# Vision tower on one core: the front rebuilt with one half ahead, one sum of squares for two norms, and attention with 88-token value chunks

## The chip, the cores and the metric

The kernel runs on one core of one Trainium2 chip. The metric is device time in microseconds (us), lower is better.

## The reference, cut to what matters

```
h = patches @ W + b + pos, two class tokens in front        # 8 images, S = 66 tokens, D = 192
a = layernorm(h)                                            # "complex" attention, 12 heads of 16
sr = (qr kr' + qi ki') / 4 ; si = (qi kr' - qr ki') / 4
h = h + softmax(sqrt(sr*sr + si*si)) @ v
x = layernorm(h); r = x                                     # the encoder's input
for i in range(4):                                          # 4 layers
    nx = rmsnorm(r, ln1[i])
    q, k, v = nx @ attn_q[i], nx @ attn_k[i], nx @ attn_v[i]    # 12 heads of 64
    r = r + softmax(q k' + bias) @ v @ attn_o[i]
    nx = rmsnorm(r, ln2[i])
    y = relu(nx @ ffn_wi[i]) @ ffn_wo[i]                    # inner width 768
    if i in (1, 3): y += top-2 mixture of 8 experts (gelu)
    r = r + y
out = h + rmsnorm(r, ln_f)
```

## The kernel before, in words

All state lies transposed, features on partitions, tokens along the row. The 8 images are two halves of 4 images (264 tokens), and the halves leapfrog: while one half does softmax, the other half gives TensorE products. Every fp32 product of a weight with an activation is made of five fp32r products (`split_pairs`): weights and activations are split in a high and a low part. The weights come from HBM in chunks (`split` stages): SyncE loads `raw`, ScalarE writes the high part (`high_part`), GpSimd the low part (`low_parts`, three or four pieces), and only then may TensorE use the chunk.

What is done when is written out by hand in `stages()`, one list of stages. Each of the five engines walks through the same list and does its own part of every stage, strictly in that order. So an engine that waits in one stage also holds up its own part of all the later ones. PSUM banks are handed around in list order as well: three banks `pa` (copied out by ScalarE), three `pd` (by VectorE), two `ps` (scores); the hidden products of the feed-forward (`hid`) take `pa` and `ps` banks, which VectorE frees.

The stages that matter here, each for a half `hf` and mostly for one image `b`:

- `cproj`, `cscores`, `croot`, `cexp`, `ctp`, `cvals`, `cpv`: projection, the two score parts and their squares, root and maximum, exponential with sum and scale, transpose, values, and product with the values, all of the complex attention in the front.
- `mean`, `squares`, `norm`, `scale`: a norm. `squares` is ScalarE's, `norm` sums the squares on TensorE (12 tiny products), VectorE adds epsilon, GpSimd takes the power -0.5 (`inverse_root`), and `scale` spreads the root over the partitions on TensorE, after which VectorE scales and splits x (`split_x`).
- `qk` (six product groups for q and six for k), `scores`, `tp`, `pv`, `o_tail`, `o_main`: attention of a layer. The softmax of one image takes VectorE (bias added to two halves of the heads, maximum), GpSimd (maximum subtracted), ScalarE (exponential, `exps`), VectorE (sum and reciprocal), GpSimd (scaled), TensorE (`tp`), in this order. In a `scores` stage for b > 0 the exponential, the sum and the scaling are those of image b - 1; `scores_end` does them for the last image.
- `v`: the values, made with tokens on partitions: `xs` as the stationary operand, 66 tokens of one image, and 384 columns of the weights stream past, 10 products an image; ScalarE copies them to `vtok`.
- `logits`: the router of the mixture, a chain of some 25 short VectorE instructions.
- `warm(n)`: n products of zeros on TensorE where it would be idle otherwise.

The front does both halves of each step one after the other and ends with both attention outputs; then layer 0 begins. The encoder's layernorm and the first `ln1` norm are two norms in series. In the layers without experts (0 and 2) both halves' attention is interleaved image by image (`scores`, `pv`, `v`, with `warm(2)`). In layers 1 and 3 each half does `scores` and `v` of its four images alternately, then `hid`, then `tp` and `pv` among parts of the other work.

## Time and profile before

| what | us |
|---|---|
| median of 3 runs | 766.58 (756.33 to 770.01) |
| the profiled execution, its own time | 758.47 |
| its span, first to last instruction | 755.7 |
| TensorE matmul busy | 704.8 (93%) |
| TensorE weight load busy | 626.9 (83%) |
| VectorE busy | 445.1 (59%) |
| ScalarE busy | 406.6 (54%) |
| GpSimd busy | 352.2 (47%) |
| mean granted TensorE clock | 0.972 of full speed |

Matmul busy counts pipelined instructions from start to end, so 93% does not mean peak speed, and it includes the 191 `warm` products, which compute nothing. Time is lost where the order makes an engine wait; the rows further down show the stretches.

### The profile page before, as it was taken

What the parts mean: (1) busy time and instruction counts of PE and PEld (TensorE: products, weight loads), DVE (VectorE), ACT (ScalarE), POOL (GpSimd) and SP (SyncE); (2) the same over time, 40 slices, a digit from 0 to 9 for tenths busy, and PEclk for the clock granted to TensorE, in tenths of its full rate; (3) what the DMA queues carried; (4) which work ended last, traced back from release to release, by engine and by line L of the source; (5) the groups of instructions that cost most, each with busy time, mean ns of one, the idle gap of its engine ahead of it and who ended that gap; (6) DMA issues with size and microseconds to landing.
All of it is one profiled execution on the core that took longest, in us unless ns stands there. A gap on an engine that the chain in (4) does not pass through costs nothing.

```text
span 755.7 us, 16388 instructions
## 1 busy us (share of the span) xinstructions
PE 704.8 (93%) x6735; PEld 626.9 (83%) x6735; DVE 445.1 (59%) x941; ACT 406.6 (54%) x913; POOL 352.2 (47%) x327
## 2 busy tenths in 40 slices
PE   6976999899899999899999999998999999999995
PEld 4853578788787989899999888887889898999995
DVE  0348435386556486676556645764765865666664
ACT  1387335542456365677767355444554647767642
POOL 2357525472466244336675333515743533544520
PEclk9997899998999999999999999989999999999998
DMA  7321001020220204243345030002211134233200
GB/s 211 88 74 43 2 2 33 1 85 1 69 78 18 59 3 131 81 126 116 119 143 147 3 84 1 2 2 74 74 43 33 28 105 123 83 116 91 89 1 22
DMA packets 36609, 49.20 MB, mean 65 GB/s; under 512 B 6155, under 2 KB 27575, under 8 KB 36023
## 3 DMA queue, kind: packets, MB, share of 16 engines
q1 hardware_dynamic: 33259, 43.49, 20.1%
q10 hardware_dynamic: 3276, 4.67, 2.0%
q8 instruction: 53, 0.87, 0.5%
q14 instruction: 21, 0.17, 0.1%
HBM read 47.70 MB, written 0.45 MB: 64 GB/s over the span
## 4 chain that ended last, share of the span: by engine, by line
PE 72%; DVE 9%; ACT 8%; POOL 5%; issue 3%; DMA 2%; SPq 0%; POOLq 0%; ACTq 0%; DVEq 0%
PE pd L684 35%; PE pa L684 23%; PE ps L684 9%; PE pa L715 4%; POOL w L613 1%; DVE xn L1102 1%; POOL prob L622 1%; ACT wide L1022 1%; POOL wo L613 1%; ACT w L934 1%; ACT wqkv L934 1%; DVE xs L1072 1%; DVE xs L1074 1%; ACT pa L1023 1%; ACT csq L983 1%
## 5 line engine op out<-in xcount | busy, mean ns | idle before, releaser
L613 POOL TENSOR_TENSOR w<-raw,w 128x384 fp32r<-128x384 f32 x140 | 141.8, 1015 | 132.0 <-ACT w L934 124.1
L684 PE MATMUL pd<-wide,w 128*128 128x264 f32 x1200 | 156.0, 286 | 0.1
L684 PEld LDWEIGHTS pd<-wide,w 128*128 128x128 f32 x1200 | 149.2, 188 | 0.9 <-DVE wide L1250 0.9
L684 PE MATMUL pa<-xs,w 128*128 128x264 f32 x810 | 120.7, 289 | 10.3 <-DVE wide L1250 6.6
L684 PEld LDWEIGHTS pa<-xs,w 128*128 128x128 f32 x810 | 107.1, 190 | 14.9 <-DVE wide L1250 8.6
L1250 DVE TENSOR_TENSOR wide<-pa,wide 128x264 fp32r<-128x264 f32 x144 | 62.1, 432 | 40.4 <-ACT pa L1023 38.0
L622 POOL TENSOR_TENSOR prob<-prob,mx 66x792 f32<-66x792 f32 x36 | 55.4, 1543 | 45.9 <-DVE mx L1062 45.6
L1022 ACT ACTIVATE wide<-pa 128x264 fp32r<-128x264 f32 x144 | 56.8, 394 | 35.0 <-PE pa L684 34.8
L628 POOL TENSOR_TENSOR prob<-prob,rc 66x792 f32<-66x792 f32 x36 | 54.4, 1513 | 44.1 <-DVE rc L1068 44.1
L684 PE MATMUL ps<-xs,w 128*128 128x264 f32 x480 | 74.3, 285 | 0.5 <-DVE prob L1227 0.5
L613 POOL TENSOR_TENSOR wqkv<-raw,wqkv 128x384 fp32r<-128x384 f32 x48 | 49.6, 1034 | 48.0 <-ACT wqkv L934 45.2
L1138 DVE TENSOR_TENSOR pd<-pd,vtok 128x264 f32<-128x264 f32 x64 | 43.6, 681 | 39.5 <-PE pd L684 39.4
L684 PE MATMUL pa<-xs,wqkv 128*128 128x264 f32 x480 | 61.7, 287 | 4.7 <-DVE xs L1074 4.0
L684 PEld LDWEIGHTS ps<-xs,w 128*128 128x128 f32 x480 | 64.6, 188 | 1.3 <-issue 1.2
L684 PEld LDWEIGHTS pa<-xs,wqkv 128*128 128x128 f32 x480 | 59.3, 188 | 7.6 <-DVE xs L1074 6.6
L684 PE MATMUL pa<-wqkv,xs 128*66 128x384 f32 x320 | 63.5, 345 | 0.0
L684 PE MATMUL pd<-warm_x,warm_w 128*128 128x512 bf16 x191 | 59.2, 429 | 0.0
L902 ACT ACTIVATE qk<-pa 128x264 f32<-128x264 f32 x102 | 39.4, 390 | 36.8 <-PE pa L684 36.5
L634 POOL TENSOR_TENSOR rs<-var,exponent 88x3 f32<-88x3 f32 x22 | 18.7, 849 | 85.6 <-DVE var L1084 85.6
L1023 ACT ACTIVATE pa<-pa 128x264 f32<-128x264 f32 x144 | 56.6, 393 | 0.0
L934 ACT ACTIVATE w<-raw 128x1536 fp32r<-128x1536 f32 (+1 forms) x40 | 52.6, 1321 | 7.4 <-PE pd L684 3.9
L1006 ACT ACTIVATE vtok<-pa 66x384 f32<-66x384 f32 x64 | 29.8, 482 | 46.5 <-PE pa L684 46.4
(126 smaller groups left out, 1149.4 us busy)
## 6 DMA issues: line engine op xcount, KB each, us to landing
raw<-in_moe_w_dram SPq DMA_DIRECT2D x16, 576.0 KB, 4.2
raw<-in_moe_w_dram SPq DMA_DIRECT2D x16, 384.0 KB, 3.5
raw<-in_moe_w_dram SPq DMA_DIRECT2D x32, 192.0 KB, 3.9
vtok<-cw_rows ACTq DMA_DIRECT2D x4, 1056.0 KB, 6.0
raw<-in_attn_o_dram SPq DMA_DIRECT2D x4, 576.0 KB, 4.0
raw<-in_ffn_wo_dram SPq DMA_DIRECT2D x4, 576.0 KB, 4.1
vtok<-in_patches_dram SPq DMA_DIRECT2D x2, 768.0 KB, 7.9
raw<-in_attn_q_dram SPq DMA_DIRECT2D x4, 384.0 KB, 3.6
```

Source lines behind the costliest of these rows:

```text
L613: ins = nc.gpsimd.tensor_tensor(low, whole, high.bitcast(F32), ALU.subtract)
L622: nc.gpsimd.tensor_tensor(p, p, m.unsqueeze(2).to_broadcast([S, H, S]), ALU.subtract).then_inc(sub_ready, 1)
L628: nc.gpsimd.tensor_tensor(p, p, r.unsqueeze(2).to_broadcast([S, H, S]), ALU.mult).then_inc(prob_ready, 1)
L684: return nc.tensor.matmul(out_ap, lhsT, rhs, start=first, stop=last)
L715: last = nc.tensor.transpose(bank[0:S, j * S:(j + 1) * S], probs(u)[:, g * HG + j, :], ident[0:S, 0:S])
L902: nc.scalar.activation(dst, src, ACT.Copy).then_inc(a_free, 1)
L934: nc.scalar.activation(hi, src, ACT.Copy).then_inc(chunk_hi, 1)
L1006: nc.scalar.activation(vtok[0:S, hf * HALF_B + b, n * F // 2:(n + 1) * F // 2], bank_a()[0:S, 0:F // 2], ACT.Copy).then_inc(a_free, 1)
L1022: nc.scalar.activation(wide[hf][:, 0, m, :], bank, gate_fn)
L1023: nc.scalar.activation(bank, bank, gate_fn).then_inc(h_ready, 1)
L1138: done(nc.vector.tensor_tensor(part, part, weight, ALU.mult))
L1250: nc.vector.tensor_tensor(wide[hf][:, 1, m, :], places["h"][n][0][:, 0:NT], wide[hf][:, 0, m, :].bitcast(F32), ALU.subtract).then_inc(h_fr ...
```

## The change

1. Scores: the products of the two 64-row groups (even and odd heads) now alternate, one from each, into two banks, where before six of one group were followed by six of the other.
2. Values: 3 chunks of 88 tokens (`VCN`) for a half instead of 4 images of 66 tokens. ScalarE copies a chunk to a staging tile (`v_rows`), waits for its copies, and issues two DMAs that carry the rows to their images in `vtok`; `pv` waits for `v_moved`. Staging lies over `wide` (half 0) or `qk` (half 1), and half 1's q and k lie over its `wide` (`qk_late`).
3. Norm: the encoder's layernorm and the `ln1` of layer 0 use one sum of squares; the variance of the second follows from that of the first. GpSimd takes both roots in one stage, x goes through `sq`, and the copy `h1T` moves from ScalarE to GpSimd.
4. Front: the raw complex weights have a place of their own, so SyncE loads the first two weight chunks at once, and their `split` stages come before `cproj`. A small Sqrt at the start brings ScalarE's table in, and a `sqrt_table` stage does so once more. Half 0 goes through the whole complex attention first; half 1's scores come after it and the rest of half 1's (`croot` 2 and 3, `cexp`, `ctp`, `cpv`, norm) in layer 0.
5. Order in the layers: `scores` stages are spread out between `v`, `qk` and `hid`; in the expert layers `scores` of image 3 comes after `logits` (half 1) or after the first `tp` (half 0), and `scores_end` after the `w1` split. The `warm` products fall from 191 to 93: layers 0 and 2 from 32 each to 14 and 11, layers 1 and 3 from 18 to 13, the front from 91 to 42.
6. Small: gate and value weights are doubled onto all 128 rows and halved by ScalarE; `cvals` is one stage an image.

The diff, cut to its core:

```diff
@@ the expert layers, half 1 (half 0 is similar)
-        for b in range(HALF_B):
-            yield ("scores", 1, layer, b)
-            if b == 0:
-                yield ("scale", 0, "ln2", layer)
-            yield ("v", 1, layer, b)
-        yield from hid(0, layer, 0)
+        yield ("scores", 1, layer, 0)
+        yield ("v", 1, layer, 0)
+        yield ("scale", 0, "ln2", layer)
+        yield ("v", 1, layer, 1)
+        yield ("scores", 1, layer, 1)
+        yield ("v", 1, layer, 2)
+        yield ("hid", 0, layer, 0, 0)
+        yield ("scores", 1, layer, 2)
+        yield ("hid", 0, layer, 0, 1)
         yield ("logits", 0, layer)
         yield ("tp", 1, layer, 0)
-        yield ("scores_end", 1, layer)
+        yield ("scores", 1, layer, 3)
         yield ("split", None, "w1", layer, 1)
         yield ("cw_out", 0, layer)
         yield ("y_tail", 0, layer, 0)
         yield ("pv", 1, layer, 0)
         yield ("tp", 1, layer, 1)
+        yield ("scores_end", 1, layer)
@@ layer 2 (layer 0 from its second block of half 1 on)
+                yield from qk(0, layer)
+                yield ("scores", 0, layer, 0)
+                yield ("v", 0, layer, 0)
+                yield ("norm", 1, "ln1", layer)
+                yield ("v", 0, layer, 1)
+                yield ("scores", 0, layer, 1)
+                yield ("scale", 1, "ln1", layer)
+                yield ("v", 0, layer, 2)
+                yield ("scores", 0, layer, 2)
+                yield ("qk", 1, layer, 0)
+                yield ("tp", 0, layer, 0)
+                yield ("scores", 0, layer, 3)
+                yield ("pv", 0, layer, 0)
+                yield ("qk", 1, layer, 1)
+                yield ("tp", 0, layer, 1)
+                yield ("scores_end", 0, layer)
+                yield ("pv", 0, layer, 1)
...
@@ PE, scores
-                    for g in range(2):
-                        bank = bank_s()
-                        row = slice(DK * g, DK * g + DK)
-                        for j in range(HG):
-                            last = mm(bank[0:S, j * S:(j + 1) * S], qk[row, 0, j, cols], qk[row, 1, j, cols], True, True)
-                        last.then_inc(s_full, 1)
+                    pair = [bank_s(), bank_s()]
+                    for j in range(HG):
+                        for g in range(2):
+                            row = slice(DK * g, DK * g + DK)
+                            last = mm(pair[g][0:S, j * S:(j + 1) * S], qk_of[hf][row, 0, j, cols], qk_of[hf][row, 1, j, cols], True, True)
+                            if j == HG - 1:
+                                last.then_inc(s_full, 1)
@@ ACT, v
+                    rows_of = v_rows(hf, layer)
                     for n in range(2):
-                        nc.scalar.activation(vtok[0:S, hf * HALF_B + b, n * F // 2:(n + 1) * F // 2], bank_a()[0:S, 0:F // 2],
+                        nc.scalar.activation(rows_of[:, c, n * F // 2:(n + 1) * F // 2], bank_a()[0:VCN, 0:F // 2],
                                              ACT.Copy).then_inc(a_free, 1)
+                    act.wait_ge(a_free, groups_after(A_GROUPS, stage))
+                    for b, to, at, rows in V_MOVES[c]:
+                        act.dma_start(vtok[to:to + rows, hf * HALF_B + b, :], rows_of[at:at + rows, c, :]).then_inc(v_moved[hf][b], 16)
@@ DVE, norm
+                if kind == "encoder":
+                    nc.vector.tensor_scalar(var_enc[:, :], sums, EPS_LN, None, ALU.add)
+                    nc.vector.tensor_scalar(var[:, :], sums, 1.0 + EPS_RMS, EPS_RMS * EPS_LN, ALU.mult, ALU.add).then_inc(d_free, 1)
```

## Rows read from the trace of the kernel before

**Rows 1.** The page, busy time, share of the span and instructions of each engine.

```profile
PE 704.8 (93%) x6735; PEld 626.9 (83%) x6735; DVE 445.1 (59%) x941; ACT 406.6 (54%) x913; POOL 352.2 (47%) x327
```

**Rows 2.** Timeline of TensorE, layer 1, half 0: start, us, what, idle before.

```profile
214.09 1.47 PE L684 MATMUL ps<-qk 64*66 64x66 f32 x24
215.49 1.95 PE L684 MATMUL pa<-wqkv,xs 128*66 128x384 f32 x10
217.37 1.47 PE L684 MATMUL ps<-qk 64*66 64x66 f32 x24
...
235.35 0.92 PE L684 MATMUL pd<-probT,vtok 66*64 66x66 f32 x24
...
244.71 0.80 PE L684 MATMUL pd<-ident,rs 88*128 88x88 f32 x6
...
246.29 1.47 PE L684 MATMUL pd<-warm_x,warm_w 128*128 128x512 bf16 x6
247.87 3.91 PE L684 MATMUL pa<-xs,wqkv 128*128 128x264 f32 x30
```

**Rows 3.** Timeline of TensorE, the front and layer 0's two ends.

```profile
75.70 1.74 PE L684 MATMUL pd<-vtok,xn 128*66 128x192 f32 x4 [4.94 <-DVE vc L1193]
...
91.51 0.67 PE L684 MATMUL pd<-probT,vc 66*32 66x66 f32 x32
...
93.95 0.71 PE L684 MATMUL pd<-hT,mean_w 128*128 128x264 f32 x2 [0.63 <-DVE hT L1216]
...
110.32 7.64 PE L684 MATMUL pa<-xs,wqkv 128*128 128x264 f32 x60
...
204.98 3.92 PE L684 MATMUL pa<-xs,wqkv 128*128 128x264 f32 x30 [1.52 <-DVE xs L1074]
```

**Rows 4.** Groups by line and form: busy us, mean ns, idle before and its releaser.

```profile
L1227 DVE TENSOR_TENSOR prob<-ps,bias 66x396 f32<-66x396 f32 x64 | 32.7, 550 | 20.5 <-PE ps L684 20.3
L1062 DVE TENSOR_REDUCE mx<-prob 66x12 f32<-66x792 f32 x36 | 34.8, 973 | 4.1 <-ACT prob L990 3.0
L1067 DVE TENSOR_REDUCE rc<-prob 66x12 f32<-66x792 f32 x36 | 34.8, 966 | 31.9 <-ACT prob L914 31.9
L622 POOL TENSOR_TENSOR prob<-prob,mx 66x792 f32<-66x792 f32 x36 | 55.4, 1543 | 45.9 <-DVE mx L1062 45.6
L613 POOL TENSOR_TENSOR w<-raw,w 128x384 fp32r<-128x384 f32 x140 | 141.8, 1015 | 132.0 <-ACT w L934 124.1
L634 POOL TENSOR_TENSOR rs<-var,exponent 88x3 f32<-88x3 f32 x22 | 18.7, 849 | 85.6 <-DVE var L1084 85.6
L914 ACT ACTIVATE prob<-prob 66x792 f32<-66x792 f32 x36 | 30.9, 863 | 24.3 <-POOL prob L622 23.8
```

**Rows 5.** Busy time by stretch (PE, PEld, DVE, ACT, POOL), granted clock, DMA.

```profile
76.00:82.00 6.00, 6.00 (x25) 2.85 (x23) 2.59 (x5) 1.75 (x3) 4.10 (x3) 0.50 0.02 4
```

**Rows 6.** The same view, later stretch, end of layer 2's attention.

```profile
501.00:506.00 5.00, 5.00 (x39) 3.34 (x39) 3.33 (x7) 0.00 (x0) 0.00 (x0) 0.56 0.02 3
```

**Rows 7.** Timeline of TensorE: first products of layers 2 and 3.

```profile
433.78 2.09 PE L684 MATMUL pa<-xs,wqkv 128*128 128x264 f32 x15 [0.29 <-DVE xs L1074]
...
522.55 3.92 PE L684 MATMUL pa<-xs,wqkv 128*128 128x264 f32 x30 [1.53 <-DVE xs L1074]
```

**Rows 8.** Timeline of ScalarE's queue, one issue of a transfer.

```profile
282.51 0.58 ACTq L1030 DMA_DIRECT2D cw_rows<-cw  x1
```

**Rows 9.** The DMA view: weight loads, KB each, median us to landing.

```profile
raw<-in_moe_w_dram SPq DMA_DIRECT2D x32, 192.0 KB, 3.9
```

**Rows 10.** Timeline of TensorE, layer 1, half 1: first scores, first expert's hid.

```profile
259.85 1.47 PE L684 MATMUL ps<-qk 64*66 64x66 f32 x24
...
290.41 0.88 PE L684 MATMUL ps<-xs,w 128*128 128x264 f32 x5
```

**Rows 11.** Timeline of VectorE: first and last instruction of a router.

```profile
278.80 0.18 DVE L1114 COPY lg<-pd 88x24 f32<-88x24 f32 x1 [0.20 <-PE pd L684]
...
282.30 0.18 DVE L1132 TENSOR_TENSOR cw<-cw,lg 88x24 f32<-88x24 f32 x1
```

More of the change, by code:

```diff
@@ L92, in stages @@
     yield ("norm", 1, "complex", 0)
-    yield from warm(6)
-    for part in range(3):
-        yield ("cproj", 0, part)
-        if part == 0:
-            yield ("scale", 1, "complex", 0)
+    yield from warm(4)
     yield ("split", None, "qkv", 0, 0)
     yield ("split", None, "qkv", 0, 1)
+    yield ("cproj", 0, 0)
+    yield ("scale", 1, "complex", 0)
+    yield ("cproj", 0, 1)
+    yield ("cproj", 0, 2)
     for b in range(HALF_B):
         yield ("cscores", 0, b)
-        if b < 3:
-            yield ("cproj", 1, b)
-        else:
-            yield ("split", None, "qkv", 0, 2)
@@ L132, in stages @@
+    yield ("cpv", 0, 2)
     yield ("ctp", 0, 3)
-    yield from warm(2)
-    yield ("cpv", 0, 2)
-    yield ("cexp", 1, 2)
-    yield from warm(2)
+    yield ("cvals", 1, 2)
+    yield ("cvals", 1, 3)
     yield ("cpv", 0, 3)
     yield ("mean", 0, "encoder")
-    yield ("cexp", 1, 3)
+    yield ("split", None, "qkv", 0, 2)
+    yield from warm(2)
     yield ("squares", 0, "encoder")
+    yield ("cscores", 1, 0)
+    yield ("norm", 0, "encoder", 0)
+    yield ("cscores", 1, 1)
     yield from warm(2)
-    yield ("ctp", 1, 0)
@@ L162, in stages @@
-    yield from warm(2)
-    yield ("cpv", 1, 2)
-    yield from warm(2)
-    yield ("cpv", 1, 3)
+    yield ("scale", 0, "ln1", 0)
+    yield ("croot", 1, 0)
+    yield ("cscores", 1, 2)
+    yield ("croot", 1, 1)
+    yield ("scale", 0, "encoder", 0)
+    yield ("cscores", 1, 3)
+    yield from warm(4)
     for layer in range(LAYERS):
@@ L174, in stages @@
                 yield ("squares", 1, "encoder")
-                beside = [[("norm", "encoder", 0)], [("scale", "encoder", 0), ("squares", "ln1")], [("norm", "ln1", 0)], [("scale", "ln1", 0)]]
-            else:
-                beside = [[("norm", "ln1", layer)], [("scale", "ln1", layer)], [], []]
-            for b in range(HALF_B):
-                yield ("scores", 0, layer, b)
-                for x in beside[b]:
-                    yield (x[0], 1) + x[1:]
-                yield ("v", 0, layer, b)
@@ new lines, in stages @@
+                yield ("scores", 0, 0, 3)
+                yield ("tp", 0, 0, 0)
+                yield from warm(3)
+                yield ("scale", 1, "ln1", 0)
+                yield ("scores_end", 0, 0)
+                yield ("split", None, "o", 0, 0)
+                yield ("pv", 0, 0, 0)
+                yield ("scale", 1, "encoder", 0)
+                yield ("qk", 1, 0, 0)
+                yield ("tp", 0, 0, 1)
+                yield from split_block(0, 0)
+                yield ("pv", 0, 0, 1)
@@ L215, in stages @@
             yield ("squares", 0, "ln1")
+            yield ("tp", 1, layer, 3)
+            yield from warm(2)
+            yield ("pv", 1, layer, 3)
             yield ("o_tail", 1, layer)
@@ L493, in x_ready_after, with roots_after @@
             return sum(x[0] == "scale" and x[2] in ("complex", "ln1", "ln2") for x in order[:order.index(stage) + 1])
+        def roots_after(norm_stage):
+            return sum(1 + (x[2] == "encoder") for x in order[:order.index(norm_stage) + 1] if x[0] == "norm")
         def bank_places():
@@ L1235, in _ @@
                 elif name == "pv":
+                    if hf == 0 and stage[3] == 0 and stage[2]:
+                        for b in range(HALF_B):
+                            dve.wait_ge(v_moved[0][b], 16 * V_PARTS[b] * (stage[2] + 1))
                     w = wide[hf][:, :, :, stage[3] * S:(stage[3] + 1) * S]
```

313 lines of the change are left out of this document (173 added, 140 removed).

## The prediction

> **What bounds the kernel now.** I read the page first: TensorE is busy 93% of the span, the next engine 59% [rows 1]. So far TensorE seems to be the bound, but the view of stretches tells another story for the front: from 76 to 82 us the granted clock is 0.50, that is the lower of its two levels, 1.2 GHz [rows 5], after 4.9 us idle [rows 3], and part of the busy time is warm products. Then I walked its timeline with the groups by line beside it. In the expert loops product follows product, and the change doesn't touch them. In attention an image costs 1.40 us of scores and 1.88 of values (the distances of the starts) [rows 2], 3.3 in all. Its softmax costs VectorE 2 x 0.55 + 0.97 + 0.97, with the reciprocal 3.3, and GpSimd 2 x 1.5 [rows 4]. So three engines are in balance there: to take work from TensorE alone shows only where the order puts something else beside the softmax.
>
> **The sum is made against the profiled execution**, 758.5 us (span 755.7). The median of the runs shown is 8.1 above it, and I add that at the end, taking the runs after to scatter as those before.
>
> **Work that TensorE loses.** Values: 10 products of 384 columns fewer in each of 8 half-layers, 1.88 each, 15.0 us [rows 2]. Scores: 24 instructions take 1.47 from start to end, with one row group after the other. The trace has no 64-row alternation; the nearest row is `pv`, 24 instructions of the same 66 columns alternating between two column groups, 0.92 [rows 2]. With that 0.55 are saved an image, 17.6 for 32. The ends are nothing (the two groups don't overlap) and the rate of `cpv`, 32 in 0.67 over four column groups [rows 3], hence 0.50 for 24 and 31 in all; I take `pv`'s, as it has two groups as well. Warm products: 98 fewer, 1.47/6 = 0.24 each at most [rows 2], 24 us; these are worth something only where nothing was waited for. Together 56 us, and the question is how much of it comes back as waiting.
>
> A rule of the Trainium skill speaks against the second term. "TensorEngine Tiling (Array Packing)", section Instruction Overhead, gives each matmul some 60 cycles of overhead and advises not to take the tiling factor from a dimension that is already small; 66 columns are such. By it alternating would save next to nothing; the rows of `pv` and `cpv` speak for overlap. It is a rival below.
>
> **Layer 2, walked stage by stage** (88.8 us from its first product to layer 3's [rows 7]). TensorE loses 8 x 0.55 for scores, 2 x 1.88 for values and 21 warm products (0.22 from start to start), 4.5, together 12.7. The order then makes it wait: `qk` of half 1 needs its scaled x, which before came 4 us or more behind `scale` (3.2 us from `scale` to `qk` where VectorE is free [rows 2], some 2 more where a maximum and a sum stand before it in VectorE's list [rows 4]), and now only a value chunk and one scores stage (2.7) lie between, 3.0; `pv` right behind its own `tp`, 0.5; the norm and the `scale` of half 0 before `hid` with less warm, 1.2 each; image 3 of half 1 now after `y`, where `o_tail` waits for VectorE to empty `pv`, 1.7. That is 7.6. In return the stretch at half clock, 501 to 506 us [rows 6], loses its 9 warm products and the small waits about it, 4.8. Net 9.9 faster. The bounds are 5 (the clock falls for the same work) and 14 (no new wait).
>
> **Layers 1 and 3.** TensorE loses 4.4 + 3.8 + 1.1 = 9.3 in each. Half 0 between 214 and 248 us: `v` 2 now needs a `pa` bank that `hid` took, and VectorE frees it only after the sum of image 0, since `scores` 1 precedes `hid` in its list; `tp` 0 likewise waits for `scores` 2's maximum and sum. I come to `tp` 0 some 1.8 us earlier than before and to scores 3 at 232.3. From there GpSimd decides: bias and maximum 2.1, subtract 1.5, scaling of image 2 1.5, `w1` split 4 x 1.02 (in the list now ahead of `scores_end`), scaling of image 3 1.5, root 0.85 [rows 4], which ends at 243.9. The scale before stood at 244.7 [rows 2]. So a gain of 0.7 of the 4.7 removed. Half 1, from the first scores to the first expert's `hid` 30.6 us before [rows 10]: scores 3 now stands behind the router on VectorE, 3.7 us [rows 11], then bias, maximum and sum 3.3, and GpSimd again does subtract, scale, `w1` split and scale, 8.6. My walk ends at 293.3 against 290.4, so 2.9 slower. A layer with experts is 2.2 slower, both 4.4. The bounds are 5 faster and 5 slower each: the longest chain runs over five engines, and 3 us of its links are waits that I could only place to within a microsecond.
>
> **The moves of the values.** 48 DMAs on ScalarE's queue, 0.58 each to issue [rows 8], behind a wait for its own copies: 1.2 us an image chunk in which the exponentials and bank copies queued behind on ScalarE stand still. It is in the walks above (exponentials 1.1 later). A move is up to 66 rows of 3,072 bytes, 203 KB; loads of 192 KB land in 3.9 [rows 9]. Between a chunk's issue and its first `pv` lie 4 to 10 us in every half, so it costs nothing at 3.9, and at twice that about 2 us in each of 8 half-layers.
>
> **The front.** Half 0's first `qk` begins at 110.3 before, and its `mean` at 93.95 [rows 3]. Walked anew: the two high parts (2 x 1.4) leave ScalarE's way ahead of the first squares, 2.4 gained; four images of scores, squares, root and maximum take 2.5 each on ScalarE and VectorE, until 46; then exponentials and sums of half 0 alone, scale 1.5 each on GpSimd, `tp` and `pv` among projections of half 1, until 66.8, which is 27 before the old 93.95. From the mean to `qk` one norm instead of two: squares, 12 sums, variance, root 0.85, 5.5 in all. `qk` at 77.7, 32.6 earlier. Against it: between 38 and 75 us TensorE has short bursts, and [rows 5] show half clock around such work; some 15 us of products there can take twice their time, most hidden behind ScalarE. I set 6 us for it and for two-input VectorE operations beside GpSimd. With this 26.6.
>
> **Layer 0**, 94.7 before [rows 3]. It loses 4.4 + 3.8 + 18 x 0.22 = 12.2 and half 1's second norm; it gets half 1's roots, exponentials, transposes and products (5.2 on TensorE). GpSimd must subtract and scale half 1's images before the first `ctp`: about 5 us of TensorE idle behind `v` 0, another 1.5 at half 1's norm. I walk it to 89.7, so 5.0 gained. The front's work for half 1 is thus paid here in part; both together 31.6.
>
> **Sum.** 26.6 + 5.0 + 9.9 - 4.4 = 37.1 faster. 758.5 - 37.1 = 721.4 for an execution like the profiled one, 729.5 beside the median; as two of three runs before lie high and more may lie low after, I say 728.
>
> **The rivals.**
> (a) The layers with experts gain too: the waits that I placed behind the router and the `w1` split hide in what TensorE still has. Then 5 a layer instead of -2.2, 14 more: 714. For it: the walk's waits of 1 to 3 us each all hang on the same few links. Chance 0.18.
> (b) The front gains half: ScalarE, serial through roots, copies and two table changes, or the half clock, set the pace. 16 less: 744. For it: [rows 5]; against: half 0 alone has half of the work. Chance 0.17.
> (c) The row groups don't overlap, the Trainium skill's rule of small dimensions named above. Scores stay at 1.4; of the 17.6 some 10 would have shown, in layers 0 and 2 and some elsewhere: 738. Chance 0.10.
> (d) Slower: the moves land late. `pv` and all that is queued behind it on TensorE and VectorE wait in 8 half-layers; the slack is about 5 us beyond 3.9, so it decides above 9, and each further us costs 8. The gain is gone at 9 + 37/8 = 13.6 us, and at 15 the kernel is 11 slower: 777. Against: the nearest transfer in size lands in 3.9 [rows 9]. Chance 0.04.
> (e) It doesn't do what it says, as the front's warm products held the clock up and their loss lowers it over both dense layers as well: 15 us of gain lost beside (b): 752. Chance 0.05.
>
> **How the numbers follow.** My forecast has 0.46, with a range of its own of 718 to 738 from the bounds above. The range 709 to 746 takes in (a), (b), (c) and leaves out some 0.2. Two per cent of 766.6 is 15.3, about what a measurement of this kernel can tell from no change: faster is below 751. That holds for the forecast, (a), (c), nearly all of (b) and half of (e): 0.88. Slower holds for (d) and the tail of (e): 0.04. The rest, 0.08, is no change.
>
> **What the profile after would show.** `scores` groups of 24 at some 0.9 us instead of 1.47; value products x240; the first `qk` near 80 us; layer 1's first near 173; layer 2's length near 79; layer 1's no shorter than before, with TensorE waiting for GpSimd's scaling before `tp` of image 3, right behind the `w1` split; `v_moved` waits nowhere. I am wrong if layers 1 and 3 shorten by over 3 us each, if the first `qk` comes after 90, or if the granted clock is low in the dense layers over long stretches.

## The result, and the profile after

The kernel after takes 782.17 us (median of 4 runs, 780.09 to 790.22) where the kernel before takes 765.95: ratio 1.027, 95% interval 1.015 to 1.040. So it is slower, clear of no change; whether by 2% or more the interval leaves open. The forecast was 728. Executions of one program differ by 1 to 2%, and the profiled ones of experiments 1 and 7 were among the slower of theirs (spans 770.3 and 754.2). The profiled execution of after took 781.9 with a span of 780.1, 24.4 above the span of before, at a mean granted clock of 0.905 (0.972 before). The page's first part, to be laid beside [rows 1]:

```profile
PE 695.9 (89%) x6533; PEld 635.8 (82%) x6533; DVE 443.0 (57%) x941; ACT 398.4 (51%) x898; POOL 351.8 (45%) x329
```

TensorE is busy only 9 us less, although it has 202 instructions fewer and each scores stage is shorter: part of what was removed came back as products at the lower clock. And for 33 us more of the span it is idle. The view of stretches shows where, cut at the first `qk` of each layer: front, layer 0, 1, 2, 3 with the output. Columns: busy us of PE, PEld, DVE, ACT, POOL, granted clock, DMA share, GB/s. First before:

```profile
0.00:110.32 110.32, 90.78 (x895) 62.86 (x896) 47.66 (x87) 53.15 (x94) 51.31 (x57) 0.91 0.26 72
110.32:204.98 94.66, 88.08 (x907) 75.34 (x905) 52.84 (x100) 42.92 (x86) 45.34 (x38) 0.95 0.11 33
204.98:433.78 228.80, 220.91 (x2021) 207.77 (x2021) 145.24 (x328) 138.83 (x328) 118.46 (x111) 1.00 0.30 87
433.78:522.55 88.77, 83.84 (x882) 72.08 (x882) 52.69 (x98) 39.92 (x82) 37.48 (x30) 0.96 0.10 28
522.55:755.70 233.15, 221.24 (x2034) 208.89 (x2034) 146.71 (x332) 131.73 (x323) 99.59 (x92) 0.99 0.24 68
```

and after:

```profile
0.00:82.18 82.18, 68.65 (x654) 52.00 (x655) 39.70 (x71) 43.64 (x82) 40.73 (x52) 0.94 0.35 96
82.18:197.98 115.80, 99.89 (x1036) 88.16 (x1035) 61.06 (x115) 49.57 (x95) 55.96 (x46) 0.78 0.14 41
197.98:440.92 242.94, 221.89 (x1993) 209.64 (x1992) 144.12 (x328) 137.02 (x324) 118.32 (x111) 0.94 0.30 88
440.92:532.98 92.06, 82.02 (x846) 73.33 (x846) 52.38 (x97) 37.77 (x78) 37.36 (x30) 0.85 0.15 45
532.98:780.10 247.12, 223.42 (x2011) 212.71 (x2009) 145.78 (x332) 130.45 (x319) 99.42 (x92) 0.93 0.24 71
```

The front is 28.1 us shorter (forecast 26.6). Layer 0 is 21.1 longer (forecast 5.0 shorter), layers 1 and 3 are 14.1 and 14.0 longer (2.2 each), layer 2 is 3.3 longer (9.9 shorter).

**Layer 0** first. TensorE's timeline behind the second value product of half 0 (answers to [rows 3]):

```profile
98.14 1.53 PE L781 MATMUL pa<-ident,vtok 66*66 66x66 f32 x12 [4.92 <-POOL vtok L689]
99.61 1.62 PE L750 MATMUL ps<-qk 64*66 64x66 f32 x24
101.16 1.11 PE L750 MATMUL pd<-probT,vc 66*32 66x66 f32 x32
102.19 1.53 PE L781 MATMUL pa<-ident,vtok 66*66 66x66 f32 x12
103.48 3.22 PE L750 MATMUL pa<-wqkv,xs 128*88 128x384 f32 x10
106.63 0.67 PE L750 MATMUL pd<-probT_late,vc 66*32 66x66 f32 x32
107.23 0.88 PE L781 MATMUL pa<-ident,vtok 66*66 66x66 f32 x12
108.04 0.94 PE L750 MATMUL ps<-qk 64*66 64x66 f32 x24
```

and the same place by stretches:

```profile
92.00:97.00 5.00, 1.23 (x8) 0.77 (x6) 4.90 (x9) 3.50 (x5) 4.83 (x4) 0.90 0.00 0
97.00:102.00 5.00, 3.86 (x68) 3.56 (x68) 3.17 (x7) 3.15 (x5) 4.54 (x4) 0.50 0.19 54
102.00:107.00 5.00, 5.00 (x58) 4.08 (x53) 2.53 (x5) 1.75 (x4) 3.98 (x3) 0.58 0.01 3
```

TensorE waits 4.9 us for half 1's first scaled image, and then works at a granted clock of 0.50, that is 1.2 GHz. The price stands in the upper fence, as each group occurs at both levels: scores 1.62 and 0.94, transposes 1.53 and 0.88, `cpv` 1.11 and 0.67; the value products take 3.22 here and 1.95 elsewhere. The five groups from 98 to 107 us lose 3.7. "PE busy 5.00" at a clock of 0.50 is thus half of what it looks like. The same comes at 117 to 127, 162 to 177 and 192 to 197 us of this layer, each time behind a wait (1.6, 2.2 and 1.4 us). In before's layer 0, 16 of 19 stretches of 5 us show 1.00.

**Layer 1, half 0** (answers to [rows 2]). ScalarE:

```profile
210.88 1.59 ACTq L1079 DMA_DIRECT2D vtok<-v_rows_wide  x2
...
214.52 1.56 ACTq L1079 DMA_DIRECT2D vtok<-v_rows_wide  x2
216.13 0.86 ACT L981 ACTIVATE prob<-prob 66x792 f32<-66x792 f32 x1 [1.64 <-issue]
```

VectorE:

```profile
217.03 0.97 DVE L1142 TENSOR_REDUCE rc<-prob 66x12 f32<-66x792 f32 x1 [1.95 <-ACT prob L981]
218.03 0.22 DVE L1143 RECIPROCAL rc<-rc 66x12 f32<-66x12 f32 x1
218.18 0.36 DVE L1331 TENSOR_TENSOR wide<-ps,wide 128x264 fp32r<-128x264 f32 x1
```

TensorE:

```profile
207.18 0.94 PE L750 MATMUL ps<-qk 64*66 64x66 f32 x24
...
219.03 3.44 PE L750 MATMUL pa<-wqkv,xs 128*88 128x384 f32 x10 [3.23 <-DVE wide L1331]
...
227.54 0.85 PE L781 MATMUL pa<-ident,prob 66*66 66x66 f32 x12 [2.20 <-DVE wide L1331]
...
248.55 4.47 PE L750 MATMUL pa<-xs,wqkv 128*128 128x264 f32 x30
```

Read these three against time: the second pair of moves holds ScalarE until 216.1, the exponential starts then, the sum on VectorE waits for it, and behind the sum stand the operations that free `hid`'s banks, which the next value products need. From the first scores to half 1's `qk` it is 41.4 us, before 33.8. A pair of moves costs 1.56 to 1.59, 0.79 an issue, against the 0.58 of [rows 8]; in layer 0 single pairs take up to 2.23.

**Layer 1, half 1** (answers to [rows 10]). GpSimd, then TensorE:

```profile
287.83 4.21 POOL L674 TENSOR_TENSOR w<-raw,w 128x384 fp32r<-128x384 f32 x4
292.01 1.51 POOL L689 TENSOR_TENSOR prob<-prob,rc 66x792 f32<-66x792 f32 x1
```

```profile
293.57 1.53 PE L781 MATMUL pa<-ident,prob 66*66 66x66 f32 x12 [3.47 <-POOL prob L689]
...
295.88 1.59 PE L750 MATMUL pd<-probT,vtok 66*64 66x66 f32 x24
```

The last transposes wait behind the `w1` split, as forecast, and the clock falls there too. The first expert starts 36.3 us behind the first scores (261.13 to 297.40), before 30.6.

### The profile page after: what moved, and what is told of

Read it like the earlier page. It is cut to its first block, busy times and chain, and to the rows that moved or that the text cites. A ratio compares the mean times of both kernels' runs of the same rounds, so it can differ in the third digit from the quotient of the medians.

```text
span 780.1 us, 16044 instructions
## 1 busy us (share of the span) xinstructions
PE 695.9 (89%) x6533; PEld 635.8 (82%) x6533; DVE 443.0 (57%) x941; ACT 398.4 (51%) x898; POOL 351.8 (45%) x329
## 4 chain that ended last, share of the span: by engine, by line
PE 57%; DVE 13%; ACT 10%; POOL 7%; ACTq 4%; issue 4%; DMA 3%; SPq 0%; POOLq 0%; DVEq 0%
PE pd L750 28%; PE pa L750 18%; PE ps L750 7%; PE pa L781 3%; ACTq L1079 3%; POOL w L674 2%; DVE rc L1142 2%; DVE mx L1137 1%; DMA gate<-in_gate_w_dram 1%; ACT prob L981 1%; POOL prob L689 1%; DVE prob L1305 1%; ACT wide L1097 1%; POOL wqkv L674 1%; DVE hT L1233 1%
## 5 line engine op out<-in xcount | busy, mean ns | idle before, releaser
L750 PE MATMUL pa<-xs,w 128*128 128x264 f32 x810 | 124.8, 295 | 9.1 <-DVE wide L1331 5.8
L750 PEld LDWEIGHTS pa<-xs,w 128*128 128x128 f32 x810 | 110.8, 196 | 14.5 <-DVE wide L1331 7.8
L750 PE MATMUL ps<-xs,w 128*128 128x264 f32 x480 | 78.0, 294 | 1.6 <-DVE prob L1305 1.6
L1097 ACT ACTIVATE wide<-pa 128x264 fp32r<-128x264 f32 x144 | 56.6, 393 | 39.8 <-PE pa L750 37.8
L750 PE MATMUL pa<-xs,wqkv 128*128 128x264 f32 x480 | 68.1, 303 | 8.0 <-DVE xs L1149 5.2
L750 PEld LDWEIGHTS pa<-xs,wqkv 128*128 128x128 f32 x480 | 65.4, 205 | 10.3 <-DVE xs L1149 6.5
L750 PEld LDWEIGHTS ps<-xs,w 128*128 128x128 f32 x480 | 68.1, 198 | 2.3 <-issue 1.8
L674 POOL TENSOR_TENSOR wqkv<-raw,wqkv 128x384 fp32r<-128x384 f32 x48 | 49.1, 1023 | 29.4 <-ACT wqkv L1001 26.6
L750 PE MATMUL pa<-wqkv,xs 128*88 128x384 f32 x240 | 50.1, 357 | 6.7 <-DVE wide L1331 5.5
L1305 DVE TENSOR_TENSOR prob<-ps,bias 66x396 f32<-66x396 f32 x64 | 33.3, 560 | 39.9 <-PE ps L750 39.8
L1012 ACT ACTIVATE sq<-hT 128x528 f32<-128x528 f32 x16 | 10.3, 645 | 88.2 <-DVE hT L1223 88.2
L1331 DVE TENSOR_TENSOR wide<-ps,wide 128x264 fp32r<-128x264 f32 x96 | 41.3, 430 | 19.3 <-ACT ps L1098 17.7
## 6 DMA issues: line engine op xcount, KB each, us to landing
vtok<-qk ACTq DMA_DIRECT2D x8, 198.0 KB
```

Source lines behind the costliest of these rows:

```text
L674: ins = nc.gpsimd.tensor_tensor(low, whole, high.bitcast(F32), ALU.subtract)
L750: return nc.tensor.matmul(out_ap, lhsT, rhs, start=first, stop=last)
L1097: nc.scalar.activation(wide[hf][:, 0, m, :], bank, gate_fn)
L1305: nc.vector.tensor_tensor(prob[:, b, heads, :], bank_s()[0:S, 0:HG * S].rearrange("p (h n) -> p h n", h=HG), bias[:, heads, ::-1], ALU.add ...
L1331: nc.vector.tensor_tensor(wide[hf][:, 1, m, :], places["h"][n][0][:, 0:NT], wide[hf][:, 0, m, :].bitcast(F32), ALU.subtract).then_inc(h_fr ...
```

## The experiments

The forecast had named waits and the clock as what could go wrong, and had charged the moves with little. The theories tested: **clock** (fewer zeros and more waits put TensorE at the lower clock), **order** (the new order of the lists makes it wait), **moves** (staging and moving the values costs more than 80 products). Ratios are to the kernel before, run on the same chip; the experiments ran on four chips, so across the groups 1 to 8, 9 to 12, 13 to 15 and 16 to 18 the ratios tell more than the times.

**1. Zeros where the kernel after waits.** 220 of them, 55, 60, 45 and 60 in the four layers; the first of layer 0:

```
                 yield ("cexp", 1, 3)
+                yield from warm(20)
                 yield ("ctp", 1, 0)
```

> The changed kernel with 220 more products of zeros (313 instead of 93), put where TensorE waits in its layers. Theory clock (the removed products and the new waits let the granted clock fall to its lower level over the attention stretches, 70 us of half-rate loss by the stage table): the mean clock comes back from 0.905 to 0.96 or more and the time falls from 782 to 745 or less. Theory order (the chains through VectorE and GpSimd set the time, the clock only follows): the added products hide nothing and the time stays within 1% of 782 or rises.

764.1 us, ratio 1.006 (1.002 to 1.010): 18 less than after by work that computes nothing. Layer 0 takes 111.0 (115.8), layer 2 86.1 (92.1), at a clock of 0.97 instead of 0.85. The clock is part of the cause, but not all of it: the forecast of this theory was 745, and layer 1 stays at 239.8 with its clock back at 0.99.

**2. Fewer zeros in the kernel before.** 50 of its 191 taken away, in its layers, such as

```
-            yield from warm(6)
             yield from qk(1, layer)
```

> The kernel before with 50 of its 191 products of zeros taken from its layers (141 left), nothing else changed. Theory clock: the clock falls in layers 0 and 2 and the time rises by 5 to 20 us though work is removed. Theory order: the products were either hidden or on the path, so the time is the same or up to 10 us lower.

757.6, ratio 0.993 (0.989 to 0.997), layer clocks 0.96, 1.00, 0.98, 0.98. These 50 zeros weren't what kept the clock up; in this order, without long waits, they are superfluous.

**3. Only the alternating scores, in the kernel before.**

```
+                    pair = [bank_s(), bank_s()]
+                    for j in range(HG):
+                        for g in range(2):
+                            last = mm(pair[g][...], ...)
```

> The kernel before with the score products alternating between the two row groups, nothing else. If they overlap as they do in the changed kernel (24 in 0.94 us instead of 1.47), 17 us of TensorE time go; theory clock expects less than 10 of them to show, as shorter bursts bring more waiting and perhaps a lower clock; theory order expects 5 to 12, as VectorE needs 3.3 us an image and TensorE then 2.8.

757.1, ratio 0.989 (0.986 to 0.993). A scores stage takes 0.94, as forecast (0.92), but of 17 us of shorter stages some 8 show in the time (5 to 11 by the interval). The profiled executions don't show where: the four layers together are 1.4 us shorter there, layer 1 228.2 for 228.8. That the softmax of the same image takes up the rest is argued from the order and not shown.

**4. The kernel after with layers 1 to 3 in the order and with the zeros of before.** Front, layer 0, 88-token values, moves and scores stay.

> The changed kernel (new front, new layer 0, 88-token values, alternating scores, shared norm) with layers 1 to 3 in the order of the kernel before and their products of zeros back (124 in all). Theory order: layers 1 and 3 come back to 228 to 233 us or less each and layer 2 to 85 or less, time 745 to 755. Theory moves (the wait and two issues of 1.6 us a chunk on ScalarE's queue cost more than the products that they save): layers 1 to 3 stay slower than before by 3 us or more each.

The zeros are 124 in all. 754.9, ratio 0.989 (0.985 to 0.993): 27 less than after. Layers 230.1, 91.0, 234.7; layer 0 still 114.0 at a clock of 0.78.

**5. The kernel after without moves** (values by image, copied straight to `vtok`):

```
-VC, VCN = 3, NT // 3
+VC, VCN = HALF_B, S
```

> Kernel after, but the values are computed as before, an image of 66 tokens at a time, and copied straight to their place: 80 products of 384 columns more, no staging and none of the 48 moves. If the moves (two issues of 1.56 us a pair on ScalarE, and waits behind them) cost more than the products they save, it comes out 8 to 15 us faster than after, about 770, with layers 1 and 3 at 238 each. If the order alone is what costs, TensorE's 15 us of products are added back and it takes 782 to 795.

772.7, ratio 1.012 (1.005 to 1.018). It has 15 us of products more and is 9 us faster. Layer 1, half 0, from the first scores to half 1's `qk`: 35.1 (after 41.4). In layer 3 the same stretch didn't get shorter: 38.2 (after 37.8).

**6. Experiments 4 and 5 together.**

> The kernel after with layers 1 to 3 in the order of before (the fourth experiment, 754.9 us) and in addition the values by image without moves. That experiment differs from the kernel before with alternating scores, in layers 1 to 3, by the 88-token chunks and their moves alone. If the moves cost: layers 1, 2 and 3 fall from 230.1, 91.0 and 234.7 to 228, 88 and 233, and the whole to about 749. If they cost nothing and the products are dear, 755 to 765.

749.3, ratio 0.982 (0.975 to 0.989). Layers 227.6, 86.7 and 232.8, so the moves cost 2.5, 4.3 and 1.9 there. Only the last two are clear of scatter: with nothing changed in them, layer 1 took 227.6 to 230.8 and layer 2 83.9 to 88.3 (at clocks of 1.00 to 0.94) in experiments 11, 12, 14, 17 and 18. Against the fifth, the order of layers 1 to 3 with its zeros is worth 23 us.

**7. The fourth with 55 zeros more, all in layer 0.**

> The fourth experiment (new front and new layer 0, old order in layers 1 to 3) with 55 products on zeros more, all in layer 0, where TensorE waits there: 20 of them ahead of the first transposes of half 1's complex attention, where it idles 3.8 us and then shows a granted clock of 0.50 for 10 us. If the low clock is what makes layer 0 take 114 us, it falls to 104 or less and the whole to 745. If the waits themselves (for GpSimd and VectorE) set its length, it stays at 110 or more and the clock alone rises.

748.8, ratio 0.980 (0.973 to 0.987). Layer 0 110.6, clock 0.89: 3 to 6 us back of the 20, the clock mostly repaired. The stretch up to half 1's `qk` takes 40.1 at a clock of 0.97, in the fourth 45.6 at 0.76. (The wait of 3.8 in the expectation is the idle part of one window of 5 us; the row of the fourth's trace has 4.92.)

**8. The fourth with real work in the wait**, `("v", 0, 0, 1)` moved ahead of `("ctp", 1, 0)`.

> The fourth experiment with one stage moved: in layer 0 the second chunk of half 0's values (about 3 us of TensorE's work) stands ahead of the first transposes of half 1's complex attention, into the wait for GpSimd of 3.8 us, instead of behind them. If the idle time is what lowers the clock, that wait shrinks below 1.5 us, the stretch at 0.50 behind it goes, and layer 0 takes 108 instead of 114. If not, the clock stays low there and layer 0 gains at most 2.

756.0, ratio 0.992 (0.988 to 0.997). A miss. Nothing gained:

```profile
96.20 1.10 PE L776 MATMUL pa<-wqkv,xs 128*88 128x384 f32 x5 [1.10 <-ACT v_rows_first L1101]
99.16 0.54 PE L807 MATMUL pa<-ident,vtok 66*66 66x66 f32 x6 [1.86 <-POOL vtok L715]
100.86 0.87 PE L807 MATMUL pa<-ident,vtok 66*66 66x66 f32 x6 [1.17 <-ACT v_rows_first L1101]
```

The products' bank copies stand behind the exponentials on ScalarE, so the wait of 4.9 became three of 4.1 in all, and the clock is 0.50 from 102 to 117 us. Layer 0 takes 117.1.

**9. The kernel after, its moves issued by SyncE.**

```
-                    act.wait_ge(a_free, groups_after(A_GROUPS, stage))
-                    for b, to, at, rows in V_MOVES[c]:
-                        act.dma_start(...)
...
+                elif stage[0] == "v":   # in SyncE's program
+                    sp.wait_ge(a_free, groups_after(A_GROUPS, stage))
+                    for b, to, at, rows in V_MOVES[c]:
+                        sp.dma_start(...)
```

> Kernel after, with one thing changed: the 48 moves of the values are issued by SyncE, at the same place of the order, and not by ScalarE. Bytes, landing and all else stay. If the moves cost because ScalarE stands still for their issue (1.56 us a pair) and the exponentials and copies queued behind come late, the 6.3 us that half 0 of layer 1 is longer than without moves go (41.4 to 36 or less), and the whole is at or below the 772.7 of the kernel without moves: 765 to 773. If they cost because they land late, nothing changes: 780 to 784.

769.3, ratio 1.013 (1.006 to 1.020). The same as the fifth within the intervals, with all moves made: the issue on ScalarE was the price and not the landing. (SyncE, which loads the weights, now follows the list too, so a load can stand behind a chunk's copies.) The exponential that began at 216.13 in after begins at 212.19 here, counted from the first scores 2.9 earlier, and

```profile
215.93 1.95 PE L760 MATMUL pa<-wqkv,xs 128*88 128x384 f32 x10 [1.20 <-DVE wide L1338]
```

waits 1.2 where it waited 3.2, and runs at the full clock. It begins 9.8 behind the first scores instead of 11.9. Half 0 takes 37.5, and 36.4 in layer 3.

**10. The sixth with the new order in half 1 of layers 1 and 3 alone** (`hid` between the scores, scores 3 behind the router, `w1` split ahead of the end of the scores).

> The sixth experiment (old order in layers 1 to 3, values by image, 749.3 us) with half 1's attention in layers 1 and 3 alone in the order of after: hid between the scores, scores 3 behind the router, the w1 split ahead of the end of the scores. The trace of the fifth experiment has 34.5 us from half 1's first scores to the first expert against 30.0 in the sixth. If that stretch alone makes the difference, each expert layer is 4.5 to 7 longer here: 234 and 239, the whole 759 to 763. If half 0's order is what costs, both stay within 2 of 227.6 and 232.8.

760.5, ratio 1.000 (0.997 to 1.004), 11 more than the sixth (1.8% by the ratios); layers 1 and 3 are 234.9 and 240.0, which is 7.3 and 7.2 longer. The last wait, at the `w1` split:

```profile
281.94 0.88 PE L809 MATMUL pa<-ident,prob 66*66 66x66 f32 x12 [2.28 <-POOL prob L717]
```

**11. The sixth with the second half of layer 0 in the old order.**

> The sixth experiment with layer 0 changed from half 1's second norm on: half 1's qk in one piece, scores, transposes and values one image after another with zeros ahead, the tail as before, as in layer 2 of before. If the new order of this part is what lengthens layer 0 (the granted clock is 0.50 from 122 to 132, 162 to 177 and 187 to 197 us there), layer 0 falls from 116.1 to 108 or less and the whole to 741. If half 1's complex attention ahead of it is what costs, it stays at 114 or more.

747.9, ratio 0.982 (0.976 to 0.989), layer 0 115.4: no change in the sum, but two changes that cancel. From half 1's `qk` on it takes 66.8 (72.0 in the sixth, 65.8 in before). The stretch ahead of it takes 48.6 (44.1): the edit also moved the split of the output weights ahead of `qk`, beside VectorE's work on half 1's x, and the clock is low there. So the new order does cost in this part, and this run doesn't clear it.

**12. The eleventh with 26 zeros in layer 0's first part.**

> The eleventh experiment with 26 products on zeros more in the first part of layer 0: 20 ahead of the first transposes of half 1's complex attention, 6 ahead of its norm. If each long wait is followed by a stretch at the lower clock and zeros prevent it, layer 0 falls by another 4 to 6 us, to 104, and the whole to 737. If zeros only stand in the way, it is no faster than the eleventh.

741.6, ratio 0.973 (0.966 to 0.980): faster than both kernels. Layer 0 110.8, clock 0.91; up to half 1's `qk` 42.7, in the eleventh 48.6. The stretches that stood at 0.90, 0.50 and 0.58 in after:

```profile
92.00:97.00 5.00, 4.93 (x37) 2.89 (x35) 4.73 (x7) 4.97 (x8) 3.75 (x3) 1.00 0.00 0
97.00:102.00 5.00, 4.39 (x85) 3.05 (x84) 4.33 (x9) 2.74 (x5) 5.00 (x4) 1.00 0.00 0
102.00:107.00 5.00, 5.00 (x118) 4.04 (x116) 3.13 (x8) 3.49 (x7) 4.53 (x4) 1.00 0.02 3
```

**13. The kernel after, roots first.** `croot` 2 and 3 of half 1 ahead of half 0's first `qk`, its first two `cexp` between the parts of `qk`.

> Kernel after, with four stages moved in layer 0: the roots of half 1's complex images 2 and 3 ahead of half 0's first qk, and the exponentials of its images 0 and 1 between the two parts of qk, not behind its scores. On ScalarE they then don't stand behind the 12 copies of qk, which end at 90.3 us in the trace of after; VectorE and GpSimd are idle 6.8 and 8.8 us for them. If layer 0 is long because half 1's chain (root, maximum, subtraction, exponential, scale, transposes) starts behind qk's copies, the wait of 4.9 us before the first transposes goes, with it the clock of 0.50 from 97 to 107 us, and layer 0 takes 109 or less instead of 115.8, the whole 772 to 776. If the chain's own work sets the end, or the clock falls anyway, layer 0 stays above 113.

782.9, ratio 1.027 (1.020 to 1.034); layer 0 116.3. A miss: the wait of 4.9 is gone, and 0.8 and 1.9 in `qk` (its copies now stand behind roots and exponentials) and 3.7 before `cpv` are there instead.

**14. The same in the twelfth.**

> The twelfth experiment (741.6 us, layer 0 110.8 at a mean clock of 0.91) with the same four stages moved. If the chain's late start is the cause, layer 0 takes 104 to 107 and the whole 735 to 738. If not, 740 to 743.

746.2, ratio 0.981 (0.972 to 0.989); layer 0 115.2, longer than the twelfth's 110.8. Refuted here as well.

**15. The fourteenth with 88-token values, moved by SyncE.**

> The fourteenth experiment with the values in 88-token chunks again and their moves issued by SyncE: 80 value products of 384 columns fewer (15 us of TensorE), and the wait for a landed move before the product with the values. In the order of after this was 3.4 us faster than no moves (769.3 against 772.7). If the moves cost only by their issue on ScalarE, it is 3 to 8 faster than the fourteenth. If they also land late for the old order, or TensorE's saved time turns into idle time and a lower clock, it is the same or up to 5 slower.

745.9, ratio 0.983 (0.975 to 0.992), the same as the fourteenth. TensorE is busy 9 us less (670.8 for 679.9) and nothing of it shows in the times; the layers of the profiled executions are each 0.4 to 0.5 us shorter. So even with the moves off ScalarE the 88-token chunks are worth nothing that can be measured here. (The 3.4 us of the expectation compare two chips; by their ratios, 1.013 and 1.012, the ninth and the fifth don't differ.)

**16. The kernel after, less work in GpSimd's list.** For half 1's complex images it subtracts the maximum from one head of twelve:

```
+                if HALF_B <= u < B:
+                    nc.gpsimd.tensor_tensor(p[:, 0:1], p[:, 0:1], ...)
+                    return
```

> Kernel after, with GpSimd's subtraction of the maximum cut to one head of twelve for half 1's four complex images; the other heads' exponentials are taken without it (the weights are the same, as the maximum cancels). GpSimd loses 4 x 1.4 us, three of them between the roots of images 2 and 3 and the first transposes; TensorE's work stays. If half 1's chain over four engines sets the length of layer 0's first part (45 us from the first qk to half 1's qk, with 4.9 us idle ahead of the first transposes), that part is 3 to 5 us shorter and the stretch at a clock of 0.50 behind it shrinks: layer 0 at 109 to 112, the whole 776 to 779. If the low clock alone is the cause, and it falls whatever the wait, layer 0 stays at 115 to 116.

780.4, ratio 1.021 (1.016 to 1.026), layer 0 114.9, the wait 4.82. The subtractions are not what is waited for: the first image's scaling stands in GpSimd's list behind the subtraction of half 0's first scores.

**17. The same in the twelfth.**

> The twelfth experiment (741.6 us, layer 0 110.8 us) with the same cut. There zeros hold the clock at 1.00 until 117 us, so that only the chain is left to shorten: if the chain sets the end, layer 0 takes 106 to 108 and the whole 737 to 739; if TensorE's own work does (20 zeros stand in its list ahead of the transposes, 4.3 us), it stays at 110 to 111.

741.3, ratio 0.972 (0.964 to 0.979); as the twelfth within the scatter, layer 0 108.4, 2.3 shorter in one profiled execution.

**18. The twelfth with the split of the output weights behind half 1's `qk`, and `scores_end` with it.**

> The twelfth experiment with the split of the output weights in layer 0 moved from ahead of half 1's qk to behind it. In the twelfth's trace GpSimd's split (3.48 us) runs at 122.2 to 125.6, beside VectorE's three operations that make half 1's input parts: they take 1.44, 1.10 and 1.13 us there, and 0.52, 0.43 and 0.43 in the trace of after, where GpSimd is idle. If the two engines hold each other up, the three fall back to 1.4 together, the wait of 2.1 before half 1's qk goes, and layer 0 is 2 us shorter: 739.5. If not, 741 to 742.

744.2, ratio 0.974 (0.968 to 0.979); no gain. The two subtractions fell back from 1.10 and 1.13 to 0.43 each, the cast stayed at 1.44, since a scaling on GpSimd now ran beside it. The wait before `qk` stayed (2.40), but `qk` came earlier, 40.1 behind the first one (42.7). Layer 0 is nevertheless 115.2, 4.4 longer. SyncE may load a chunk only when an earlier one is split, so it issues the load of the next feed-forward weights at 138.32, ScalarE's high part waits for them, the copies of the values stand behind it, and TensorE waits for these:

```profile
142.26 1.16 ACT L1064 ACTIVATE w<-raw 128x1152 fp32r<-128x1152 f32 x1 [7.57 <-DMA raw<-in_ffn_wo_dram]
143.85 0.87 PE L843 MATMUL pa<-ident,prob 66*66 66x66 f32 x6 [7.29 <-ACT vtok L1137]
```

## Why the prediction was wrong, step by step

Between the forecast (37.1 faster than the profiled execution of before) and the measured span (24.4 longer) lie 61.5 us: layer 0 has 26.1 of them, layer 2 13.2, layers 1 and 3 11.9 and 11.8, and the front was 1.5 better than forecast.

**The front: right.** 28.1 against 26.6. `mean` begins at 66.94 (forecast 66.8), the first `qk` at 82.2 (77.7 before the reserve of 6). The printed terms between the two come to 5.5 and the times to 10.9, so half of that stretch was never listed; it took 15.2, part of it at the lower clock. Rival (b), that it gains half, is out, and so is (a), that the expert layers gain. Rival (e), the front's missing zeros as cause of a low clock in the dense layers, had the sign right (layer 2 at 0.85 for 0.96) and not the cause: with the new front and the old order, layer 2 is at 0.96 again (6).

**Work that TensorE loses: right in kind, worth far less.** Scores by `pv`'s rate: 0.94 measured, 0.53 of 1.47 saved, and rival (c) is refuted. The section Instruction Overhead of the Trainium skill's "TensorEngine Tiling (Array Packing)", from which I had it, advises against a tiling factor from a dimension that is already small. In this case the factor came from the 64 rows and not from the 66 columns, so I had applied it to the wrong dimension. But the 17.6 brought some 8 (experiment 3), the 15.0 of the values nothing measurable (15), and 50 of the zeros had been superfluous in the old order (2).

**The moves, "1.2 us an image chunk": the first failed step.** It is 1.56 to 1.59, and the mistake was less the 0.4 than the list behind it: the exponential, which I had charged as 1.1 later, VectorE's sum, and then `hid`'s bank frees. Without the moves (5) or with their issue on SyncE (9) the kernel is 9 to 13 us faster. Rival (d) had named a slower kernel, by late landing; the landing was not it (9), so that its direction came true was luck.

Half 0 of layer 1 was to be 0.7 shorter and is 7.6 longer (41.4 for 33.8). How much of that is the wait itself, experiment 16 shows, whose program doesn't differ from after's in this layer:

```profile
219.01 1.96 PE L753 MATMUL pa<-wqkv,xs 128*88 128x384 f32 x10 [3.23 <-DVE wide L1334]
...
244.09 3.90 PE L753 MATMUL pa<-xs,wqkv 128*128 128x264 f32 x30 [0.76 <-DVE xs L1152]
```

The first scores begin at 207.17, as in after, and the waits of 3.23 and 2.20 are there to the hundredth. But the value products behind the wait run at the full clock (1.96, in after 3.44), and the half takes 36.9. So 3.1 of the 7.6 are the new order and the moves, and 4.5 are what the clock took behind the same waits. The 37.5 of the ninth experiment and the 35.1 of the fifth hold such stretches as well, so the moves can't be priced from one half of one execution; the 9 to 13 us are read from whole times.

**Half 1 of layers 1 and 3, "2.9 slower": the mechanism was right, the size was not.** It was to lose this by scores 3 behind router and split, and lost 5.7 and 5.0 up to the first expert. Alone the order of half 1 costs 7.3 a layer (10): 5.2 up to the first expert (35.2 against 30.0) and the rest beyond it, where the first expert's groups run at the lower clock (1.47 for 0.88 in the sixth, 0.77 in the steady loop). The bound of 5 for a layer was too narrow since it had no price for what the clock does behind a wait.

**Layer 2, "9.9 faster": wrong.** 3.3 slower. The moves have some 2.7 of it (5) and the order as much (5 against 6), though an unchanged layer 2 differs by up to 4.4 among the later experiments. The failed term is the 4.8 for the stretch at half clock "in return": it had the wrong sign (clock 0.96 before, 0.85 after). With 45 zeros in its waits the layer keeps a clock of 0.97 and takes 86.1 (1), 6.0 less. So the waits, which I summed to 7.6 by their lengths, cost more than that by the clock behind them.

**Layer 0, "5.0 gained": the largest miss, 26 us.** The wait of 5 for GpSimd was right (4.92). The sum as printed isn't whole: 94.7 less 12.2 plus 11.7 is 94.2, and the other 4.5 down to 89.7 stand for half 1's second norm, which has no price in it. The layer falls in two parts at half 1's `qk`, first in before, then in after:

```profile
139.20 7.54 PE L684 MATMUL pa<-xs,wqkv 128*128 128x264 f32 x60 [0.65 <-DVE xs L1074]
```

```profile
127.01 5.29 PE L750 MATMUL pa<-xs,wqkv 128*128 128x264 f32 x30
```

From the first `qk` to this one my terms come to some 36 (28.9 before, less scores, values and zeros, plus 5.2, 5 and 1.5), the second norm not yet taken off; it took 44.8 (82.18 to 127.01). The groups at half clock in it lose 3.7 (above) and, in the same way, 4.1 between 118.7 and 127, about as much as the difference of 8.8. Zeros in the waits get half of it back: 40.3 at a clock of 0.97 instead of 44.8 at 0.77 (1), and 40.1 instead of 45.6 (7 against 4). For the rest other waits appear.

Behind it my terms come to some 59 (65.8 before, less four scores, a value chunk and eleven zeros); it took 71.0, at a clock of 0.79 (0.92 before). In this part the old order is 5.2 faster (11). So the step that failed is that a wait was priced at its length. Behind it products ran at half speed, and I had listed this as "wrong if" and charged nothing for it outside the front. For the first part the zeros show this, for 4.5 to 5.5 us; for the second part it is argued from the clock.

One of the second part's waits is for a load. In before the output weights are split right behind half 0's `qk`, and SyncE issues the next load at 122.72, 12.4 behind that `qk`. In after the split comes late and the load is issued at 132.67, 50.5 behind it; ScalarE waits 2.1 us for it and TensorE 2.27 for the copies behind. Experiment 18 makes this wait 7.3. I had left the place of this split out of the walk.

**What stays open.** With zeros in its waits layer 0 has its clock back (0.78 to 0.91) and is only 3 to 5 us shorter (1, 7, 12), because other waits appear. An earlier start of half 1's chain (13, 14), GpSimd's work in it (16, 17) and value products in the wait (8) are each not the cause alone. The place of the output weights' split costs on either side: ahead of half 1's `qk` it runs beside VectorE's work on x (12), behind it the next load comes late (18). No run has it where before has it. Some 16 us over before remain in the best kernel. I had charged 11.7 for the moved work of half 1, and no run took layer 0 apart further. Front and layer 0 together are 7.0 shorter than before in after (198.0 for 205.0) and 12.1 in the twelfth.

**The sum.** In ratios: the moves 1.5%, give or take as much (after to 5), the order of layers 1 to 3 with its zeros 3.0% (5 to 6), and of it 1.8% half 1 of the layers with experts (10). Without both the change is 1.8% faster than before, and 2.7% with the second half of layer 0 in the old order and zeros in the first (12).

## What to carry to other kernels

Price a new wait on TensorE at its length and add, as a second number with a chance, what may run behind it at half clock; in this case such groups took 1.7 to 1.9 times their time (scores 1.62 for 0.94, `hid` 1.47 for 0.77), and half a layer with the same waits took 41.4 or 36.9. Work removed from an engine is worth nothing until you can say which list reaches its next step earlier for it; here 17 us of shorter scores were worth some 8, and 15 us of value products nothing measurable. And when a transfer is put on a compute engine's queue, follow what stands behind the issue across two further engines before you call it hidden. When a weight chunk's place in the list moves, look at the load that waits for its slot.

## What the runs showed of the hardware

**The clock behind the same wait.** In layer 1 of after and of experiment 16 TensorE waits 3.23 us at the same place of the same program; behind it ten value products took 3.44 and 1.96.

**The same front.** It is the same program in after and in experiments 5 and 10, and took 82.2, 87.7 and 78.6 us, with the clock that the execution was granted. After stands above; these are 5 and 10:

```profile
0.00:87.70 87.70, 74.06 (x654) 56.59 (x655) 39.74 (x71) 43.99 (x82) 40.73 (x52) 0.87 0.34 90
```

```profile
0.00:78.58 78.58, 63.51 (x650) 49.07 (x655) 36.70 (x69) 42.00 (x79) 39.14 (x51) 1.00 0.37 101
```

At a clock of 1.00 it comes out within 1 us of the 77.7 that were walked for it. A stretch of this length in one profiled execution can be off by 9 us, and its granted clock has to be read with it.

**VectorE beside GpSimd.** VectorE makes half 1's high and low parts of x in the twelfth, while GpSimd scales until 122.2 and then splits until 125.7:

```profile
121.06 1.44 DVE L1203 CAST xs<-sq 128x528 fp32r<-128x528 f32 x1
122.53 1.10 DVE L1204 TENSOR_TENSOR xs<-sq,xs 128x264 fp32r<-128x264 f32 x1
```

against after, where GpSimd's scaling ends at 125.4 and nothing follows until 128:

```profile
125.22 0.52 DVE L1147 CAST xs<-sq 128x528 fp32r<-128x528 f32 x1
125.77 0.43 DVE L1148 TENSOR_TENSOR xs<-sq,xs 128x264 fp32r<-128x264 f32 x1
```

Beside GpSimd the cast takes 2.8 times as long and the subtraction 2.6 times. In the eighteenth, with a scaling on GpSimd until 120.7 and no split behind it, the cast (119.6 to 121.0) took 1.44 and the subtraction after it 0.43.
